# A window attention block on one core: fc2 with gelu's output as the stationary operand and tokens as output rows, and fc2's bias added by GpSimd

## The reference, cut to what matters

```python
y = _ln(x, norm1_w, norm1_b)                     # then roll by (-3, -3) and cut into windows
qkv = (win @ qkv_w.T) ...
attn = softmax(q @ k.T * scale + bias + mask)    # per window and head, 49 x 49
out = (attn @ v) @ proj_w.T + proj_b             # back to the image, roll by (3, 3)
x = shortcut + out
z = _ln(x, norm2_w, norm2_b)
z = gelu(z @ fc1_w.T + fc1_b) @ fc2_w.T + fc2_b  # 64 -> 256 -> 64
return x + z
```

## Time and profile before

| quantity | value |
|---|---|
| runs | 2225.48, 2228.99, 2226.96 us |
| time of the profiled execution | 2222.98 us |
| its span | 2221.2 us |
| TensorE (PE) busy | 2147.9 us, 97% |
| GpSimd (POOL) busy | 1770.5 us, 80% |
| VectorE (DVE) busy | 1748.1 us, 79% |
| ScalarE (ACT) busy | 1546.9 us, 70% |
| mean granted TensorE clock | 0.991 of full speed |
| fc2's products (L842) | 1024 instructions, mean 500 ns |

### The profile page before, as it was taken

How to read it: one execution, slowest core, us unless ns; L and a number is a source line. 1 busy time by engine, 2 the same in 40 slices (tenths; PEclk the granted TensorE clock), 3 DMA queues, 4 the chain that set the end, 5 groups by cost and what they waited for, 6 DMA issues and landing times.

```text
span 2221.2 us, 147938 instructions
## 1 busy us (share of the span) xinstructions
PE 2147.9 (97%) x62756; PEld 1670.2 (75%) x62756; DVE 1748.1 (79%) x3231; ACT 1546.9 (70%) x2435; POOL 1770.5 (80%) x1687
## 2 busy tenths in 40 slices
PE   4999999999999999999999999999999999999997
PEld 3777777777777777777777777777777777777775
DVE  5778887887887888788788788878878887887874
ACT  3577777677677677767767767776776777677675
POOL 5788888888888888888888888888888888888874
PEclk7999999999999999999999999999999999999999
DMA  4232322222323332332333223222223323322321
GB/s 109 64 76 76 76 75 75 76 76 74 77 75 76 75 75 76 73 78 75 76 76 74 76 74 76 75 74 76 75 75 77 73 75 75 75 76 74 77 67 35
DMA packets 178587, 165.86 MB, mean 75 GB/s; under 512 B 21144, under 2 KB 152458, under 8 KB 178074
## 3 DMA queue, kind: packets, MB, share of 16 engines
q1 hardware_dynamic: 178074, 157.60, 28.1%
HBM read 28.99 MB, written 25.77 MB: 25 GB/s over the span
## 4 chain that ended last, share of the span: by engine, by line
PE 83%; ACT 9%; issue 4%; SPq 2%; DVE 1%; DMA 1%; ACTq 0%; POOL 0%; DVEq 0%; POOLq 0%
PE O L749 13%; PE ST L735 10%; PE M L757 9%; PE S L713 9%; PE ST L729 8%; PE M L842 8%; PE M L820 6%; PE M L789 5%; PE M L805 5%; PE M L775 5%; ACT L445 5%; ACT gl L445 4%; PE M L850 3%; PE S L717 1%; SPq L274 1%
## 5 line engine op out<-in xcount | busy, mean ns | idle before, releaser
L326 POOL TENSOR_TENSOR nmd<-diag,nm 121x392 f16<-121x392 f16 x1024 | 898.3, 886 | 320.5 <-DVE nm L582 310.4
L582 DVE TENSOR_REDUCE nm<-S 121x8 f16<-121x392 f32 x1024 | 576.2, 563 | 276.2 <-PE S L713 151.9
L426 ACT ACTIVATE pT<-ST 113x392 f32<-113x392 f32 x1024 | 506.4, 495 | 309.9 <-PE ST L735 305.2
L749 PEld LDWEIGHTS O<-vx,pT 113*49 113x49 f32 x16384 | 547.5, 126 | 43.2 <-issue 3.2
L749 PE MATMUL O<-vx,pT 113*49 113x18 f32 x16384 | 521.3, 196 | 0.9 <-DVE on L592 0.9
L713 PE MATMUL S<-kp,qp 128*49 128x49 f16 x16384 | 387.7, 186 | 16.1 <-DVE nm L582 8.1
L729 PE MATMUL ST<-qp,kp 128*49 128x49 f16 x16384 | 386.6, 185 | 4.1 <-ACT pT L426 2.1
L713 PEld LDWEIGHTS S<-kp,qp 128*49 128x49 f16 x16384 | 313.4, 104 | 86.6 <-issue 60.2
L735 PE MATMUL ST<-nmd,shiftw 121*49 121x392 f16 x2048 | 356.8, 345 | 0.1
L729 PEld LDWEIGHTS ST<-qp,kp 128*49 128x49 f16 x16384 | 323.9, 103 | 13.3 <-issue 2.7
L735 PEld LDWEIGHTS ST<-nmd,shiftw 121*49 121x49 f16 x2048 | 107.9, 102 | 264.9 <-POOL nmd L326 130.7
(11 more groups left out here) (88 smaller groups left out, 3307.0 us busy)
## 6 DMA issues: line engine op xcount, KB each, us to landing
qp<-hl SPq DMA_DIRECT2D x1024, 49.0 KB
kp<-hl SPq DMA_DIRECT2D x1024, 49.0 KB
xin<-in_x SPq DMA_DIRECT2D x256, 98.0 KB
out<-res SPq DMA_DIRECT2D x256, 98.0 KB
kp<-in_c_keys SPq DMA_DIRECT2D x4, 588.0 KB, 7.3
weights<-in_c_weights SPq DMA_DIRECT2D x1, 448.0 KB, 5.3
bias_t<-spread SPq DMA_DIRECT2D x2, 73.5 KB, 2.2
shiftw<-in_c_shift SPq DMA_DIRECT2D x1, 139.0 KB
```

The source lines that it names most:

```text
L326: nc.gpsimd.tensor_tensor(nmd[j % LAG][:], diag[:], nm[j % LAG][:].unsqueeze(2).broadcast_to([RM, 2 * 4, N]), ALU.mult).then_inc(s_nmd, 1)
L426: nc.scalar.activation(pT[j % LAG][:].rearrange("k w h q -> k (w h q)"), ST[0:R, j % 2, 0:HK], ACT.Exp).then_inc(s_e, 1)
L582: V.tensor_reduce(nm[j % LAG][:], S[0:RM, 0:HK].rearrange("q (h n) -> q h n", n=N), AX_X, ALU.max, negate=True).then_inc(s_nm, 1)
L749: mm = MM(O[W0 * w:W0 * w + N, (4 * p + hp) * VC:(4 * p + hp + 1) * VC], pT[j % LAG][:, w, hp, :], vx[r % RING][:, window + 2 * w, hp, :], ...
```

## The change

fc2 exchanges its operands: 49 tokens of gelu's output `gl` are stationary and the 64 output channels of a weight half are the moving columns. Its output has tokens as rows at once, in M's bank 2. ScalarE's copy, the tile `mT`, TensorE's turn back and the semaphores `s_mT` and `s_mo` go. fc2's bias comes as a second row tile beside proj's (`outb`), and GpSimd adds it in place to `xres` at k = 2, for unit d = i-2. `result` now reads bank 2, waits for fc2 and for that bias, is done for unit e at k = 5 instead of unit g at k = 0 of the next body, and the store on SP follows the spreading transfers. Each engine's program has one body less at its end.

```diff
+            def add_fc2_bias(u, r):
+                pool.wait_ge(s_z0, u + 1)
+                held = xres[r % RING]
+                nc.gpsimd.tensor_tensor(held[:], held[:], fc2b.unsqueeze(1).broadcast_to([R, UP, C]), ALU.add).then_inc(s_fb, 1)
...
+                    if k == 2 and on_chip(d):
+                        add_fc2_bias(d, m + 2)
...
-            def evac_m(u):
-                act.wait_ge(s_m, u + 1)
-                if later(u):
-                    act.wait_ge(s_mo, u)
-                nc.scalar.activation(mT[:, :, 0:N], M[:, 2, 0:HT].rearrange("c (w n) -> c w n", n=N),
-                                     ACT.Identity, bias=fc2b[:, 0:1]).then_inc(s_mT, 1)
...
             def result(u, r):
-                dve.wait_ge(s_mo, u + 1)
+                dve.wait_ge(s_m, u + 1)
+                dve.wait_ge(s_fb, u + 1)
                 if later(u, 2):
                     dve.wait_ge(s_out[r % 2], 16 * u - 16 * (r % 2))
-                V.tensor_tensor(res[r % 2][:], M[0:R, 3, :], xres[r % RING][:].rearrange("r p c -> r (p c)"),
+                V.tensor_tensor(res[r % 2][:], M[0:R, 2, :], xres[r % RING][:].rearrange("r p c -> r (p c)"),
                                 ALU.add).then_inc(s_res, 1)
...
                     if k == 0:
-                        if on_chip(g):
-                            result(g, m)
                         if on_chip(d):
                             ln2_center(d, m + 2)
...
-                    if k == 5 and on_chip(n):
-                        ln1_var(n)
+                    if k == 5:
+                        if on_chip(e):
+                            result(e, m + 1)
+                        if on_chip(n):
+                            ln1_var(n)
...
             def turn_z(u, e, a):
                 pe.wait_ge(s_z1, u + 1)
                 if on_chip(e):
-                    pe.wait_ge(s_mT, e + 1)
+                    pe.wait_ge(s_res, e + 1)
...
             def fc2(u):
                 pe.wait_ge(s_g, 2 * u + 2)
-                for c in range(2):
+                for p in range(PAIRS):
                     for h in range(2):
-                        mm = MM(M[C * h:C * h + C, 2, 0:HT], w2[:, c, :], gl[:, c, h, :],
-                                start=(c == 0), stop=(c == 1), tile_position=(0, C * h), skip_group_check=True)
+                        for c in range(2):
+                            for w in range(2):
+                                tokens = slice(N * (2 * p + w), N * (2 * p + w) + N)
+                                mm = MM(M[W0 * w:W0 * w + N, 2, C * (2 * p + h):C * (2 * p + h) + C], gl[:, c, h, tokens],
+                                        w2[:, c, :], start=(c == 0), stop=(c == 1), tile_position=(0, W0 * w),
+                                        skip_group_check=True)
                 mm.then_inc(s_m, 1)
...
-                    if k == 0 and on_chip(g):
-                        turn_back(g)
```

More of the change, by code:

```diff
@@ L60, in swin_block @@
         shiftw = sb("shiftw", [RM, 4, 3, N], F16)
-        projb = sb("projb", [R, C])
-        n1w, n1b, n2w, n2b, fc2b, lopart, cpbb1 = (vec[:, n:n + 1] for n in range(7))
+        outb = sb("outb", [R, 2, C])
+        n1w, n1b, n2w, n2b, lopart, cpbb1 = (vec[:, n:n + 1] for n in (0, 1, 2, 3, 5, 6))
         b1 = vec[:, 7:9]
+        projb, fc2b = outb[:, 0], outb[:, 1]
         cpbw1 = vec[:, 9:11]
@@ L184, in swin_block @@
         s_m = sem("s_m")
-        s_mT = sem("s_mT")
-        s_mo = sem("s_mo")
+        s_fb = sem("s_fb")
         s_res = sem("s_res")
         s_out = [sem(f"s_out{r}") for r in range(2)]
-        ZEROED = RING + 2
+        ZEROED = RING + 1
         BLANK = 4
@@ L208, in rounds @@
                     body(i + t, (FIRST + t) % 4)
-            for i in range(last, NSB + 4):
+            for i in range(last, NSB + 3):
                 body(i, i % 4)
@@ L246, in load_constants @@
             def load_constants():
-                for dst, src in ((diag, c_diag), (shiftw, c_shift), (projb, c_projb)):
+                for dst, src in ((diag, c_diag), (shiftw, c_shift), (outb, c_outb)):
                     sp.dma_start(dst[:], src).then_inc(c_const_in, 16)
@@ L276, in body @@
             def body(i, m):
-                a, n, g = i + 1, i + 3, i - 4
+                a, n, e = i + 1, i + 3, i - 3
                 if on_chip(n):
@@ L285, in body @@
                     spread_bias()
-                if on_chip(g):
-                    store(g, m)
                 if on_chip(a):
@@ L290, in body @@
                     spread_parts(a, m + 1, 1)
+                if on_chip(e):
+                    store(e, m + 1)
                 if isinstance(i, int) and i == -1:
@@ L478, in body @@
                         evac_oT(c)
-                    if k == 5 and on_chip(e):
-                        evac_m(e)
             rounds(act, body)
@@ L776, in project_qk, with room_for_v @@
                 mm.then_inc(s_qk, 1)
-            def room_for_v(u, e, g):
+            def room_for_v(u, e):
                 if on_chip(e):
@@ L839, in fc2 @@
                 pe.wait_ge(s_g, 2 * u + 2)
-                for c in range(2):
+                for p in range(PAIRS):
                     for h in range(2):
-                        mm = MM(M[C * h:C * h + C, 2, 0:HT], w2[:, c, :], gl[:, c, h, :],
-                                start=(c == 0), stop=(c == 1), tile_position=(0, C * h), skip_group_check=True)
-                mm.then_inc(s_m, 1)
-            def turn_back(u):
-                pe.wait_ge(s_mT, u + 1)
-                src = mT[:].rearrange("c w n -> c (w n)")
-                for q in range(4):
-                    mm = nc.tensor.transpose(M[0:R, 3, 2 * C * q:2 * C * q + 2 * C], src[:, 2 * W0 * q:2 * W0 * q + R],
-                                             ident[:])
-                mm.then_inc(s_mo, 1)
+                        for c in range(2):
[4 more added lines that the diff above has]
+                                        skip_group_check=True)
+                mm.then_inc(s_m, 1)
             def body(i, m):
-                a, f, c, d, e, g = i + 1, i + 2, i - 1, i - 2, i - 3, i - 4
+                a, f, c, d, e = i + 1, i + 2, i - 1, i - 2, i - 3
                 if i == -2:
@@ L870, in body @@
                     if k == 1 and on_chip(a):
-                        room_for_v(a, e, g)
+                        room_for_v(a, e)
                     if on_chip(u2):
@@ L880, in body @@
                     if k == 3 and on_chip(e):
-                        fc1_high(e, a, g)
+                        fc1_high(e, a)
                     if k == 4 and on_chip(f):
@@ L895, in body @@
                         fc2(e)
-            for i in range(-3, NSB + 4):
+            for i in range(-3, NSB + 3):
                 body(i, i % 4)
@@ L972 @@
         "x": xs, "c_vec": np.concatenate(vectors, axis=1), "c_weights": np.concatenate(matrices, axis=1),
-        "c_projb": rows(L0_conv_proj_b), "c_keys": keys, "c_diag": diag, "c_shift": shiftw,
+        "c_outb": np.stack([rows(L0_conv_proj_b), rows(L0_conv_fc2_b)], axis=1), "c_keys": keys, "c_diag": diag, "c_shift": shiftw,
     }
```

16 lines of the change are left out of this document (5 added, 11 removed).

## The result

The changed kernel takes 2290.80 us (median of 4 runs, 2290.57 to 2298.51), the kernel before 2226.36 us beside it: a ratio of 1.0306 (1.0291 to 1.0322). It is 64 us slower, where 22 us less were forecast. The profiled execution is the slowest of the runs, 2298.51 us with a span of 2296.7.

A forecast was written before the change was run, and what follows sets the result against it. TensorE was taken to bound the kernel, 128 times its program per unit. TensorE's work -27, a possible GpSimd path wait +6 and the end -1 gave -22 us, from 2226.96 to 2205 us, range 2194 to 2223.

The forecast's parts named there:

- TensorE's own work: On TensorE per unit: new fc2 1.84 us against 2.05 us removed, -0.21 us, over 128 units -27 us.
- `project_v`'s rate: Price for fc2's 64 load-and-product pairs, taken from products of the same shape: 28.8 ns per pair, 1.84 us.
- The slots: Short gaps for VectorE and GpSimd work before TensorE's `scores`: they tighten but nearly hold, 0.05 us per unit, +6 us.
- this path: Through GpSimd, from `scores` of step 7 to step 3: 7.35 us inside 7.37, wait between none and 0.18 us per unit.
- GpSimd's load per unit: GpSimd gains a 1.60 us operation: 15.3 us of a 16.5 us period, 93%, up from 82%, still under the period.
- L553 unchanged at 0.69 us: Sign on VectorE: this operation keeps its time, while GpSimd's addition or the tile beside it takes longer.
- the hold of L553: Rival: GpSimd's new addition delays this VectorE operation, `times_v` waits 0.7 us; net +0.5 us per unit, 2290 us; chance 0.07.
- -1 us at the end: Last unit, once: copy and turn back, 0.60 + 0.70 us, go; fc2's 0.49 us more comes.
- the forecast's own range: Case that the forecast itself holds: between -0.21 and -0.08 us per unit, 2197 to 2216 us; chance 0.70.

The follow-up runs named there:

- e3: Changed kernel with gelu's output in windows of 64, so fc2 has 113 stationary columns and 32 instructions instead of 64, and pairs: 2437.17 us, 1.095.
- e2: Changed kernel without GpSimd's addition of fc2's bias and its wait (output lacks that bias): 2301.35 us, 1.0354.
- e1: Kernel before with `shift` in four pieces of 98 columns, same work, 96 more TensorE instructions per unit: 2262.99 us, 1.0164.
- e8: Changed kernel with `shift` in two pieces of 196 columns, 32 more instructions: 2320.08 us, 1.0429, 29 us above the changed kernel.
- e11: Kernel before with `shift` in eight pieces of 49 columns in steps 4 to 7 alone, 112 more instructions per unit: 2280.57 us, 1.0266.
- e6: Changed kernel with `project_v` and `project_out` as two wide products each, 80 instructions fewer per unit, values and projection left out: 2217.78 us, 0.9977.
- e5: Kernel before with `project_v` and `project_out` as two wide products each, 80 instructions fewer per unit, values and projection left out: 2229.89 us, 1.0031.
- e10: Changed kernel with `gl` and a copy of fc2's weights in float16, one instruction per fc2 product instead of two: 2171.51 us, 0.9777.
- e9: Kernel before with `gl` and a copy of fc2's weights in float16, one instruction per fc2 product instead of two: 2209.55 us, 0.9948.
- e12: Kernel before with four more loads of 98 KB per unit, behind the spreading transfers, into tiles nobody reads: 2249.79 us, 1.0112.

## Why the prediction was wrong, step by step

**TensorE's own work: right.** fc2 measured 1.80 us (1.84 forecast, at `project_v`'s rate), `turn_back` left nothing behind, and the clean period is 16.42 us (16.5), 0.27 us shorter for 1.80 - 2.05 = -0.25 us of TensorE's own work. The rule of the Trainium skill on loads ("TensorE: Matmul & The Clock Gate", Part 3), by which only other row groups hide a load, would have made fc2 2.6 us or more. The measurement decides against it: 28 ns per pair with the same 128 rows in every load, as `project_v` had shown. That it is the alternating column halves that hide the loads fits e3, where every load covers both halves and a pair takes 103 ns, but is argued.

**The slots: right.** `scores` of step 3 stood at 600.07 without a wait, and from 100 to 2100 us no wait of a `scores` is put down to VectorE; so the 0.05 us per unit that the sum set aside for this path (+6 us) did not come. GpSimd's load per unit was 15.2 us (347.91 of 400 us, in a mean period of 17.46), as forecast, and 87% and not 93% only because the period grew. "L553 unchanged at 0.69 us" was wrong: the hold of L553 (now L549), a rival, exists and is covered. Its group row in ns, least, median and most, and VectorE at one of the strongest cases, beside GpSimd's addition from 424.22 on:

```profile
L549 DVE SCALAR_TENSOR_TENSOR y<-sum,xin x128: 681/943/1815, 14.6 to 2208.0; 113x512 f32<-113x512 f32 x128
```

```profile
424.25 1.78 DVE L549 SCALAR_TENSOR_TENSOR y<-sum,xin 113x512 f32<-113x512 f32 x1
425.95 0.35 DVE L584 RECIPROCAL rec<-O 113x32 f32<-113x32 f32 x1
426.34 0.42 DVE L588 TENSOR_TENSOR on<-O,rec 113x256 f32<-113x256 f32 x1
```

It was 0.69 us in the earlier trace rows. `times_v` waited for L588 only 9 times, 3.7 us in the whole run. That this rival's price met the measured time was chance: e2 takes its cause away, and the time stays.

**The failed step** is the sentence "So the time is 128 times what TensorE's program takes per unit, as long as no other engine makes it wait." It leaves out that the program itself must arrive. The working counted fc2's 64 pairs by their 28.8 ns and the turn back by its 0.70 us, but not as instructions: fc2 from 8 to 64 pairs, the turns from 4 to none, 104 more instructions per unit, 991 to 1095, in a period 0.27 us shorter. Its price is the excess, +111 us against the -35 us saved. No rival had it, although the page of the kernel before shows q8's 495 packets, 4.4 us apart on average, and 4% of "issue" in the chain. One small slip in the sums changed nothing: -0.21 us per unit and -1 us at the end give 2199 us as the lower end of the forecast's own range, not 2197.

Shown are: the waits stand at packet edges (numbering, and the landing of a packet before each); instructions alone make them (e1, e8, e11); GpSimd's addition does not (e2); with fewer instructions elsewhere the change gains (e6 against e5), and with half the instructions in fc2 it gains more (e10 against e9).

**Open.** Why the fetch of the next packet begins now 0.6 and now 2.6 us after an edge in the changed kernel, and earlier in the kernel before; why TensorE goes on no sooner than 1.18 us behind a landing; how much the spreading and the other transfers add (e12). In units 4 to 122 the changed kernel's edge waits are 107 us of 0.94 x 119 = 112 us of excess. TensorE also makes up for some of its waits in shorter distances behind them, so the near agreement of the two does not say what each single wait costs.

## What to carry to other kernels

Count instructions, not only their time: where TensorE is the bound with small products, read the instruction queue's packets beside the span, and look for stretches in which 256 instructions pass in less than about 4 us. The mean rate is a first hint only: from 64 per us on every kernel here had an excess of 0.30 us per unit or more, but so had e3 at 57. A wait put down to "issue" in the middle of a group of equal products is the sign. An exchange of operands that turns few wide products into many narrow ones pays when it is joined with what halves their number, as float16 does here: e10, at 0.9777 of the kernel before, is the version to take where float16 in fc2 is good enough.

## What the runs showed of the hardware that I had not expected

- TensorE can starve for instructions while its clock is full and the DMA engines are 29% busy: stops of up to 1.4 us, mostly behind packets whose 256 instructions would pass in under 3.7 us.
- A packet of 256 instructions takes 1.1 us in the median, its fetch begins some 1.2 us after TensorE has passed an edge, and TensorE goes on about 1.4 us behind its landing, when it stood.
- A float32 pair with 49 stationary and 64 moving columns costs 28 ns when the column halves alternate, one with 113 stationary columns 103 ns: one wide pair costs more than three narrow ones.
- A VectorE operation beside a GpSimd one on the same kind of data was held from 0.68 to 1.8 us; without that operation (e2) the hold is gone and the time is no shorter.
